# Attention and mixture-of-experts layer on one core: v is transposed by VectorE in 32x32 blocks instead of by TensorE

## The chip, the cores and the metric

One Trainium2 chip, and one of its cores. The metric is the device time of one execution in microseconds (us). The kernel before takes 1060.97 us, the median of 3 runs (1059.65 to 1061.65). The profiled execution, from which every duration below comes, took 1057.24 us; its span in the profile is 1055.5 us.

## The reference, cut to what matters

The kernel computes a layer norm, attention with rotary positions, a second layer norm and a mixture of 8 experts with top-2 routing, all in float32. The change touches only how v reaches the product with the attention weights:

```python
B, L, D = 4, 512, 256;  NQ, NKV, HD = 32, 8, 64      # 4 q heads share one k and one v
proj = layernorm(x) @ W_qkv                            # q, k, v
q, k = rope(q), rope(k);  v = v.reshape(B, L, NKV, HD)
attn = einsum('bqhmd,bkhd->bhmqk', q, k) / 8, masked
w    = softmax(concat([attn, sink]))[..., :-1]         # weights of 512 keys
out  = einsum('bhmqk,bkhd->bqhmd', w, v) @ W_out       # v has 512 rows (keys) of 64
x = x + out;  x = x + ffn(layernorm(x))                # 8 experts, 640 places each
```

## The kernel before

Attention is done in 32 groups (`g`, one batch and one k/v head each), and a group has 16 score tiles of 128 queries by 512 keys (`UNITS`). The main loop `all_periods` has one period per group, of 16 steps `n`. It is software-pipelined: at step `n` of period `g` each engine first does step `n` of group `g`, then step `n - 16` of group `g + 1` (its projection), then step `n + 16` of group `g - 1` (its product with v and its output). So a table entry of -8 stands for step 8 of the period before, and one of 24 for step 8 of the period after. The five engines run their own copies of this list in its order and meet only at semaphores.

In one period, in the order of its steps:

- **TensorE**: at each even step a pair of score tiles (line 1562, 32-bit, two halves of the array at once). A pair waits (line 1558) until VectorE has reduced all tiles but the last one of the pair before. After the pairs of steps 0 and 2 the first two of the next group's three projection chunks (line 1508), after those of steps 4, 6 and 8 the product of the previous group's weights with v (line 1586; 80, 80 and 96 matmuls), after that of step 10 the third chunk (line 1491), after those of steps 12 and 14 the output projection (line 1618).
- **VectorE**: for each tile one mask-scale-minimum instruction (line 1162), at each odd step from 3 on one 32x32-block transposition of two tiles of weights (line 1171), at step 1 the reciprocals (lines 1180 and 1184), at step 9 the division by the sums (line 1191, `heads_sb`), which waits for the last product with v.
- **ScalarE**: the exponentials (line 862), the copies of projection chunks out of PSUM (line 844, `chunk_sb`), and the output copies.
- **GpSimd**: the rotary arithmetic (lines 691, 692, 696) and the split of the weights into two parts.
- **SyncE**: the DMA queue. Per period, in order: reciprocals out and in, the swaps for the rotation of k and of the first q chunk, k doubled, the weights three groups ahead, v out to DRAM (line 505), v in (line 513), the swaps of the second q chunk.

A projection chunk `KV` holds k in partitions 0 to 63 and v in partitions 64 to 127, with one row per feature and the 512 positions along the row. The product needs v with keys in partitions, repeated in four groups of 32 partitions (`v_quads`). Before the change this goes: TensorE transposes v after the score pair of step 8 (`TURN_V_AT`, `turn_v`, line 1526: four transpositions of 64x128 into the bank PROJ); ScalarE copies the bank to `v_next` at step 9 (`v_copy`, line 852); SyncE writes `v_next` to DRAM in one DMA of 128 rows of 1 KB; it reads it back four times into `v_quads`. The third projection chunk (line 1488) waits for ScalarE's copy, since both use the bank PROJ. `v_next` also serves, as `xn1`, for a normalised tile of a later batch in 12 periods (`LATE_PERIODS`, lines 990 to 995).

In periods 0 to 5 VectorE also takes statistics of the later batches (lines 1392 and 1393), in some others the routing's small instructions (`dve_route`). The group before the first period is written out by hand (lines 896 to 916, 1374 to 1381, 1629 to 1640). After the periods, from about 800 us on, come the experts, which the change does not touch.

Of the kernel before, what the change touches and what calls it, by code (L numbers as in the profile page):

```python
# [20 lines left out]
F32 = mybir.dt.float32  # L21
# [5 lines left out]
P = 128  # L27
# [23 lines left out]
BLK = 32  # L51
# [8 lines left out]
def moe_layer(nc, x, w_qkv, w_out, sink, gate_w, w1, b1, w2, b2, rope, out):  # L60
    ctx = ExitStack()
    with ctx:
        slot_rows = nc.dram_tensor("slot_rows", (E * CAP, ROW), F32, kind="Internal").ap()

        v_rows = nc.dram_tensor("v_rows", (P, TPB * HD), F32, kind="Internal").ap()
# [111 lines left out]
        s_v_next = sem("s_v_next")  # L177
# [83 lines left out]
        v_next = sb("v_next", [P, TPB, HD], c=actx)  # L261
        qk_st.append(sb("qk_st1", [P, PAIRS + 1, L], c=actx))
        v_quads = [sb(f"v_quads{i}", [P, TPB, TPB * HD], c=actx) for i in range(2)]
# [13 lines left out]
        xn1 = v_next[:, :, :].rearrange("p t d -> p (t d)")  # L277
# [63 lines left out]
        TURN_V_AT, V_NEXT_AT = -8, -7  # L341
# [97 lines left out]
        def turned_v_bank(g):  # L439

            return PV[0] if g == 0 else PROJ

# [24 lines left out]
        def _(sp):  # L467
# [352 lines left out]
        def _(act):  # L820
# [16 lines left out]
            def chunk_out(g, c):  # L837
# [4 lines left out]
                if c == Q23 and g > 0:  # L842
                    act.wait_ge(s_v_turned, g + 1)
# [4 lines left out]
            def v_copy(g):  # L848
                act.wait_ge(s_v_turned, g + 1)
                if g > 0:  # L850
                    act.wait_ge(s_v_out, g * 16)
                nc.scalar.activation(v_next[:, :, :], turned_v_bank(g)[:, 0:TPB * HD].rearrange("p (c d) -> p c d", d=HD),
                                     ACT.Copy).then_inc(s_v_next, 1)

            def act_step(n, g, j):
                if n in CHUNK_OUT_AT:
                    chunk_out(g, CHUNK_OUT_AT[n])
                if n == V_NEXT_AT:
                    v_copy(g)
# [56 lines left out]
            v_copy(0)  # L916
# [44 lines left out]
            def act_ahead(m):  # L961
# [28 lines left out]
                if m in LATE_NORM_AT:  # L990
                    i = LATE_NORM_AT[m]
                    act.wait_ge(s_late, 1 if i < TPB else 2)
                    act.wait_ge(s_v_out, (LATE_PERIODS[i] + 1) * 16)
                    nc.scalar.activation(xn1, x_sb[:, TPB + i, :], ACT.Identity,
# [111 lines left out]
        def _(dve):  # L1106
# [49 lines left out]

            def dve_step(n, g, j):
# [18 lines left out]
                if n == RECIP_AT:  # L1176
# [7 lines left out]
                    nc.vector.transpose(recip_t[:, :], recip[:, :]).then_inc(s_recip, 1)  # L1184
                if n == HEADS_AT:
# [190 lines left out]
            rotate_q()  # L1376
            dve.wait_ge(s_mask, 1)
# [87 lines left out]
        def _(pe):  # L1465
# [16 lines left out]
            def project(g, j, c):  # L1482
# [4 lines left out]
                else:  # L1487
                    pe.wait_ge(s_v_next, g + 1)
# [25 lines left out]

            def turn_v(g):
                pe.wait_ge(s_chunk_out, g * CHUNKS + (Q01 if g > 0 else KV) + 1)
                if g % NKV == 3 and g > NKV:
                    pe.wait_ge(s_x2T, 2 * (g // NKV))
                if g % NKV == 4 and g > NKV:
                    pe.wait_ge(s_centred, g // NKV)  # L1520
                if g % NKV == 5 and g > NKV:
                    pe.wait_ge(s_place, g // NKV)
                if g - 1 in LATE_PERIODS:
                    pe.wait_ge(s_xT_lo, TPB + LATE_PERIODS.index(g - 1) + 1)
# [276 lines left out]
```

## Time and profile before

| what | value |
|---|---|
| median of 3 runs | 1060.97 us (1059.65 to 1061.65) |
| profiled execution | 1057.24 us, span 1055.5 us |
| TensorE matmul | 1024.9 us busy, 97% of the span |
| TensorE weight load | 720.9 us, 68% |
| VectorE | 926.8 us, 88% |
| ScalarE | 655.0 us, 62% |
| GpSimd | 665.1 us, 63% |
| granted TensorE clock, mean | 0.993 |
| chain that ended last | TensorE 56%, VectorE 37%, issue 3% |

Busy shares are means over the whole span; what ends a wait is read from the chain and from the timelines. The idle time of an engine is printed behind the instruction that ends it, in brackets, with what released it.

### The profile page before, as it was taken

What the parts mean: (1) busy time and instruction counts of PE and PEld (TensorE: products, weight loads), DVE (VectorE), ACT (ScalarE), POOL (GpSimd) and SP (SyncE); (2) the same over time, 40 slices, a digit from 0 to 9 for tenths busy, and PEclk for the clock granted to TensorE, in tenths of its full rate; (3) what the DMA queues carried; (4) which work ended last, traced back from release to release, by engine and by line L of the source; (5) the groups of instructions that cost most, each with busy time, mean ns of one, the idle gap of its engine ahead of it and who ended that gap; (6) DMA issues with size and microseconds to landing.
All of it is one profiled execution on the core that took longest, in us unless ns stands there. A gap on an engine that the chain in (4) does not pass through costs nothing.

```text
span 1055.5 us, 32277 instructions
## 1 busy us (share of the span) xinstructions
PE 1024.9 (97%) x12943; PEld 720.9 (68%) x12943; DVE 926.8 (88%) x1967; ACT 655.0 (62%) x1671; POOL 665.1 (63%) x607
## 2 busy tenths in 40 slices
PE   7899999999999999999999999999988999999996
PEld 4466666666666666666666666666656999999995
DVE  6999999999999999999999999999985787777773
ACT  4666667666667766667776666776663555445551
POOL 6667776777666888666787777777752333333332
PEclk9999999999999999999999999999989999999998
DMA  3534544544333334333334334333424555555521
GB/s 112 142 108 118 137 131 140 132 112 135 93 83 83 96 99 111 99 104 81 80 95 114 100 103 121 98 83 96 119 70 162 119 119 123 117 123 124 101 46 21
DMA packets 155893, 112.10 MB, mean 106 GB/s; under 512 B 76480, under 2 KB 145152, under 8 KB 155616
## 3 DMA queue, kind: packets, MB, share of 16 engines
q1 hardware_dynamic: 137680, 90.03, 33.0%
q0 software_dynamic: 7296, 8.55, 4.8%
q10 hardware_dynamic: 10768, 11.46, 3.6%
q8 instruction: 102, 1.67, 0.7%
q14 instruction: 47, 0.39, 0.1%
HBM read 74.84 MB, written 21.83 MB: 92 GB/s over the span
## 4 chain that ended last, share of the span: by engine, by line
PE 56%; DVE 37%; issue 3%; ACT 1%; POOL 1%; DMA 1%; SPq 0%; POOLq 0%; DVEq 0%; ACTq 0%
PE bank L1586 22%; DVE probs_ring L1162 16%; DVE probs_t L1171 14%; PE bank L1562 10%; PE bank L1739 9%; PE bank L1750 6%; DVE heads_sb L1191 4%; PE bank L1753 3%; PE bank L1618 1%; PE bank L1508 1%; PE bank L1526 1%; PE bank L1533 1%; DVE neg_max L1162 0%; ACT probs_ring L862 0%; PE bank L1491 0%
## 5 line engine op out<-in xcount | busy, mean ns | idle before, releaser
L862 ACT ACTIVATE probs_ring<-probs_ring,neg_max 128x512 f32<-128x512 f32 x512 | 365.8, 717 | 210.3 <-DVE neg_max L1162 209.6
L1162 DVE CUSTOM_DVE_ANT_0 probs_ring<-bank,mask,sink_neg 128x512 f32<-128x512 f32 x512 | 360.1, 737 | 26.6 <-PE bank L1562 25.5
L1171 DVE STREAM_TRANSPOSE probs_t<-probs_ring 128x1024 f32<-128x1024 f32 x256 | 317.5, 1240 | 0.2 <-ACT probs_ring L862 0.2
L1562 PE MATMUL bank<-qk_st 64*128 64x512 f32 x1024 | 281.1, 625 | 11.9 <-DVE neg_max L1162 7.4
L1586 PE MATMUL bank<-probs_t,v_quads 32*64 32x256 f32 x8192 | 247.6, 381 | 0.1
L1586 PEld LDWEIGHTS bank<-probs_t,v_quads 32*64 32x64 f32 x8192 | 179.1, 132 | 76.5 <-issue 48.8
L691 POOL TENSOR_TENSOR chunk_sb<-chunk_sb,rope_sb 128x512 f32<-128x512 f32 (+1 forms) x94 | 120.0, 1276 | 103.9 <-issue 82.7
L810 POOL DMA_INDIRECT out<-expert_sb,slots x40 | 78.8, 1969 | 143.1 <-DVE expert_sb L1428 134.5
L1562 PEld LDWEIGHTS bank<-qk_st 64*128 64x128 f32 x1024 | 85.3, 186 | 77.4 <-DVE neg_max L1162 41.8
L696 POOL TENSOR_TENSOR qk_st<-chunk_sb,swap_sb 128x512 f32<-128x512 f32 (+1 forms) x94 | 120.2, 1279 | 7.4
L1618 PEld LDWEIGHTS bank<-wo_sb,heads_sb 64*128 64x128 f32 x992 | 96.1, 187 | 37.4 <-issue 29.2
L692 POOL TENSOR_TENSOR swap_sb<-swap_sb,rope_sb 128x512 f32<-128x512 f32 (+1 forms) x94 | 120.5, 1281 | 0.0
L1077 ACT ACTIVATE hidden<-bank,b_sb 128x320 f32<-128x320 f32 x128 | 60.6, 525 | 95.7 <-PE bank L1739 95.7
L1618 PE MATMUL bank<-wo_sb,heads_sb 64*128 64x256 f32 x992 | 117.4, 376 | 0.0
L1750 PE MATMUL bank<-w_part,hidden_hi 128*128 128x512 f32 x320 | 114.1, 398 | 0.0
L1508 PE MATMUL bank<-xcur,w_hi 64*128 64x512 f32 x496 | 100.9, 481 | 0.0
L862 ACT ACTIVATION_READ_ACCUMULATOR probs_ring<-probs_ring,neg_max 128x1 f32 x512 | 97.4, 190 | 0.0
L1753 PE MATMUL bank<-w_part,hidden_lo 128*128 128x256 f32 x320 | 90.1, 282 | 0.0
L726 POOL TENSOR_TENSOR x_sb<-x_sb,y_sb 128x512 f32<-128x512 f32 x62 | 79.2, 1277 | 4.5
L1739 PE MATMUL bank<-slots_hi,w_hi 128*128 128x320 f32 x256 | 79.5, 310 | 0.5 <-DVE expert_sb L1428 0.5
L1739 PE MATMUL bank<-slots_lo,w_hi 128*128 128x320 f32 x256 | 79.0, 308 | 0.0
L1739 PE MATMUL bank<-slots_hi,w_lo 128*128 128x320 f32 x256 | 79.0, 308 | 0.0
(191 smaller groups left out, 1342.7 us busy)
## 6 DMA issues: line engine op xcount, KB each, us to landing
v_quads<-v_rows SPq DMA_DIRECT2D x128, 128.0 KB
recip_wide<-recip_rows SPq DMA_DIRECT2D x64, 256.0 KB
w_raw<-in_L_ffn_w SPq DMA_DIRECT2D x14, 1024.0 KB, 7.6
swap_sb<-chunk_sb SPq DMA_DIRECT2D x314, 32.0 KB
w_raw<-in_L_attn_W_qkv SPq DMA_DIRECT2D x32, 256.0 KB, 2.9
slot_rows<-x2T ACTq DMA_DIRECT2D x8, 662.5 KB, 5.8
slots_cut<-slot_rows SPq DMA_DIRECT2D x56, 80.0 KB, 3.0
w_raw<-in_L_attn_W_qkv SPq DMA_DIRECT2D x64, 64.0 KB, 2.7
```

The source lines that it names most:

```text
L691: nc.gpsimd.tensor_tensor(straight, straight, rope_sb[rows, 0, :], ALU.mult).then_inc(s_pool, 1)
L692: nc.gpsimd.tensor_tensor(swapped, swapped, rope_sb[rows, 1, :], ALU.mult).then_inc(s_pool, 1)
L696: nc.gpsimd.tensor_tensor(qk_st[j][rows, PAIRS if c == KV else c - Q01, :], straight, swapped, ALU.add).then_inc(s_rot, 1)
L862: nc.scalar.activation(probs[(g * UNITS + n) % RING][:, :], probs[(g * UNITS + n) % RING][:, :], ACT.Exp, bias=neg_max[j][:, n:n + 1], sca ...
L1162: nc.vector.tensor_tensor_reduce(probs[(g * UNITS + n) % RING][:, :], SCORE[SCORE_OF[n // 2][n % 2]][:, :], mask[:, L - P - t * P:2 * L - ...
L1171: nc.vector.transpose(probs_t[j][:, :, (h // 2) * (2 * P):(h // 2 + 1) * (2 * P)] .rearrange("p b (h q) -> p h b q", h=2)[:, :, :, t * BLK ...
L1562: nc.tensor.matmul(SCORE[SCORE_OF[n // 2][hh]][:, :], qk_st[j][half, h // 2, t * P:(t + 1) * P], qk_st[j][half, PAIRS, :], start=True, sto ...
L1586: ins = nc.tensor.matmul(PV[a][p * HD:(p + 1) * HD, 0:2 * P], v_quads[j][rows, d, c * HD:(c + 1) * HD], probs_t[j][rows, blk, p * 2 * P:(p ...
L1618: ins = nc.tensor.matmul(PV[a][:, 0:D], heads_sb[rows, a, h * P:(h + 1) * P], wo_sb[rows, (g % NKV) * 2 + h, :], start=(half == 0 and h == ...
L1739: ins = nc.tensor.matmul(banks[4 + 2 * (c % 2) + half][:, 0:HALF], w[:, kc, c * P:(c + 1) * P], a[:, at:at + HALF], start=(kc == 0 and m = ...
L1750: nc.tensor.matmul(FFN2[s][:, :], hidden_hi[:, c, s * P:(s + 1) * P], w2_parts[e % 2][:, c, :, :].rearrange("p t d -> p (t d)"), start=(c ...
L1753: ins = nc.tensor.matmul(FFN2[s][:, 0:D], hidden_lo[:, c, s * P:(s + 1) * P], w2_hi[e % 2][:, c, :], start=False, stop=(c == HC - 1))
```

## The change

v is transposed by one VectorE instruction in 32x32 blocks, straight from `chunk_sb[KV]` into partitions 64 to 127 of `swap_sb[KV]`, which nothing else uses. It is placed at step 6 of the period, after that step's tile. Within a block keys and features change places, while the blocks stay: a row of the result is (feature half, key within block) and holds 16 blocks of 32 features. Two DMAs, one per feature half, write it to DRAM as 32 rows (key within block) of 16 x 64, in pieces of 32 numbers. The DMAs back to `v_quads` then move 32 whole rows of 4 KB. TensorE's transposition, ScalarE's copy and their semaphore go; the waits that guarded the bank PROJ move to the third projection chunk; `xn1` becomes a buffer of its own.

```diff
-        v_rows = nc.dram_tensor("v_rows", (P, TPB * HD), F32, kind="Internal").ap()
+        v_rows = nc.dram_tensor("v_rows", (BLK, BLOCKS * HD), F32, kind="Internal").ap()
...
-        v_next = sb("v_next", [P, TPB, HD], c=actx)
+        xn1 = sb("xn1", [P, D], c=actx)
-        v_quads = [sb(f"v_quads{i}", [P, TPB, TPB * HD], c=actx) for i in range(2)]
+        v_quads = [sb(f"v_quads{i}", [P, BLOCKS, HD], c=actx) for i in range(2)]
+        v_turned = swap_sb[KV][HD:P, :]
-        TURN_V_AT, V_NEXT_AT = -8, -7
+        TURN_V_AT = -10
...
 # SyncE, v_out
-                sp.wait_ge(s_v_next, g + 1)
+                sp.wait_ge(s_v_turned, g + 1)
-                sp.dma_start(v_rows, v_next[:, :, :].rearrange("p t d -> p (t d)")).then_inc(s_v_out, 16)
+                for q in range(HD // BLK):
+                    sp.dma_start(v_rows.rearrange("j (b d) -> j b d", d=HD)[:, :, q * BLK:(q + 1) * BLK],
+                                 v_turned[q * BLK:(q + 1) * BLK, :].rearrange("j (b i) -> j b i", i=BLK)
+                                 ).then_inc(s_v_out, 16)
 # SyncE, v_in
-                sp.wait_ge(s_v_out, g * 16 + 16)
+                sp.wait_ge(s_v_out, g * 32 + 32)
-                    sp.dma_start(v_quads[j][a * BLK:(a + 1) * BLK, :, :],
-                                 v_rows.rearrange("(c j) n -> j c n", j=BLK)).then_inc(s_v_in[j], 16)
+                    sp.dma_start(v_quads[j][a * BLK:(a + 1) * BLK, :, :].rearrange("j b d -> j (b d)"),
+                                 v_rows).then_inc(s_v_in[j], 16)
 # ScalarE
-                if c == Q23 and g > 0:
-                    act.wait_ge(s_v_turned, g + 1)
+                if c == KV and g > 0:
+                    act.wait_ge(s_v_turned, g)
-            def v_copy(g):
...
-                nc.scalar.activation(v_next[:, :, :], turned_v_bank(g)[:, 0:TPB * HD].rearrange("p (c d) -> p c d", d=HD),
-                                     ACT.Copy).then_inc(s_v_next, 1)
-                    act.wait_ge(s_v_out, (LATE_PERIODS[i] + 1) * 16)
+                    if i > 0:
+                        act.wait_ge(s_norm_turned, TPB + i)
 # VectorE
+            def turn_v(g):
+                dve.wait_ge(s_chunk_out, g * CHUNKS + KV + 1)
+                if g > 0:
+                    dve.wait_ge(s_v_out, g * 32)
+                nc.vector.transpose(v_turned, chunk_sb[KV][HD:P, :]).then_inc(s_v_turned, 1)
+                if n == TURN_V_AT and g > 0:
+                    turn_v(g)
...
             rotate_q()
+            turn_v(0)
 # TensorE, project(g, j, Q23)
-                    pe.wait_ge(s_v_next, g + 1)
+                    pe.wait_ge(s_chunk_out, g * CHUNKS + Q01 + 1)
+                    if g % NKV == 3 and g > NKV:
+                        pe.wait_ge(s_x2T, 2 * (g // NKV))
...
+                    if g - 1 in LATE_PERIODS:
+                        pe.wait_ge(s_xT_lo, TPB + LATE_PERIODS.index(g - 1) + 1)
-            def turn_v(g):
...
-                for c in range(TPB):
-                    ins = nc.tensor.transpose(turned_v_bank(g)[:, c * HD:(c + 1) * HD],
-                                              chunk_sb[KV][HD:P, c * P:(c + 1) * P],
-                                              identity[HD:P, HD:P])
-                        c, d = divmod(blk, TPB)
-                                                       v_quads[j][rows, d, c * HD:(c + 1) * HD],
+                                                       v_quads[j][rows, blk, :],
```

## Rows read from the trace of the kernel before

**Rows 1.** Chain of waits, part of the page: its shares by line.

```profile
PE bank L1586 22%; DVE probs_ring L1162 16%; DVE probs_t L1171 14%; PE bank L1562 10%; PE bank L1739 9%; PE bank L1750 6%; DVE heads_sb L1191 4%; PE bank L1753 3%; PE bank L1618 1%; PE bank L1508 1%; PE bank L1526 1%; PE bank L1533 1%; DVE neg_max L1162 0%; ACT probs_ring L862 0%; PE bank L1491 0%
```

**Rows 2.** The chain in order of time: start, us on the chain, what.

```profile
366.51 0.24 PE bank L1526 x4
...
372.40 1.16 DVE probs_t L1171
...
381.33 0.71 DVE probs_ring L1162
...
382.10 1.13 PE bank L1562 x4
```

**Rows 3.** Timeline of TensorE, 358 to 367: start, us, line, idle before.

```profile
358.21 1.13 PE L1562 MATMUL bank<-qk_st 64*128 64x512 f32 x4
359.27 1.11 PE L1586 MATMUL bank<-probs_t,v_quads 32*64 32x256 f32 x30
...
365.38 1.13 PE L1562 MATMUL bank<-qk_st 64*128 64x512 f32 x4
...
366.69 2.85 PE L1586 MATMUL bank<-probs_t,v_quads 32*64 32x256 f32 x96
```

**Rows 4.** Every STREAM_TRANSPOSE of VectorE: ns min/median/max, first and last start.

```profile
L1171 DVE STREAM_TRANSPOSE probs_t<-probs_ring x256: 1233/1241/1245, 25.2 to 790.2; 128x1024 f32<-128x1024 f32 x128
...
L1184 DVE STREAM_TRANSPOSE recip_t<-recip x32: 211/211/216, 45.4 to 791.6; 128x32 f32<-128x32 f32 x32
...
L1448 DVE STREAM_TRANSPOSE slots_t<-slots_cut x7: 1503/1505/1516, 836.2 to 1005.4; 128x1280 f32<-128x1280 f32 x7
```

**Rows 5.** Timeline of VectorE: the tile of step 8 and the division, five periods.

```profile
104.83 1.42 DVE L1191 TENSOR_TENSOR heads_sb<-bank,recip_wide 128x256 f32<-128x256 f32 x4
...
272.73 1.42 DVE L1191 TENSOR_TENSOR heads_sb<-bank,recip_wide 128x256 f32<-128x256 f32 x4 [0.49 <-PE bank L1586]
...
297.10 1.42 DVE L1191 TENSOR_TENSOR heads_sb<-bank,recip_wide 128x256 f32<-128x256 f32 x4 [0.23 <-PE bank L1586]
...
345.74 1.42 DVE L1191 TENSOR_TENSOR heads_sb<-bank,recip_wide 128x256 f32<-128x256 f32 x4 [0.31 <-PE bank L1586]
...
366.54 0.75 DVE L1162 CUSTOM_DVE_ANT_0 probs_ring<-bank,mask,sink_neg 128x512 f32<-128x512 f32 x1 [0.73 <-PE bank L1562]
...
369.64 1.42 DVE L1191 TENSOR_TENSOR heads_sb<-bank,recip_wide 128x256 f32<-128x256 f32 x4 [0.51 <-PE bank L1586]
```

**Rows 6.** The chain in period 0 and at its end.

```profile
23.92 0.73 DVE probs_ring L1162
...
46.31 1.13 PE bank L1562 x4
```

**Rows 7.** Timeline of VectorE, the first score tile.

```profile
20.76 0.75 DVE L1162 CUSTOM_DVE_ANT_0 probs_ring<-bank,mask,sink_neg 128x512 f32<-128x512 f32 x1 [0.93 <-PE bank L1562]
```

**Rows 8.** DMA issues: count, KB each, median us from issue to landing.

```profile
slots_cut<-slot_rows SPq DMA_DIRECT2D x56, 80.0 KB, 3.0
...
v_rows<-v_next SPq DMA_DIRECT2D x32, 128.0 KB, 2.5
```

**Rows 9.** Timeline of GpSimd, the rotation of the second q chunk in one period.

```profile
214.26 1.29 POOL L691 TENSOR_TENSOR chunk_sb<-chunk_sb,rope_sb 128x512 f32<-128x512 f32 x1 [2.18 <-DMA swap_sb<-chunk_sb]
...
216.86 1.28 POOL L696 TENSOR_TENSOR qk_st<-chunk_sb,swap_sb 128x512 f32<-128x512 f32 x1
```

**Rows 10.** Timeline of TensorE, the score pair of step 8 in that period.

```profile
219.72 1.13 PE L1562 MATMUL bank<-qk_st 64*128 64x512 f32 x4
```

**Rows 11.** Stretches of the last period: length, busy us by engine, granted clock, DMA.

```profile
762.00:768.00 6.00, 3.44 (x20) 1.67 (x20) 5.96 (x15) 4.58 (x14) 5.14 (x7) 0.90 0.23 67
768.00:774.00 6.00, 6.00 (x86) 2.71 (x84) 3.98 (x8) 5.38 (x11) 1.52 (x2) 0.53 0.30 96
```

**Rows 12.** Timeline of TensorE in the last period, at the lower clock.

```profile
767.62 2.08 PE L1562 MATMUL bank<-qk_st 64*128 64x512 f32 x4 [1.72 <-DVE neg_max L1162]
769.63 4.36 PE L1586 MATMUL bank<-probs_t,v_quads 32*64 32x256 f32 x80
```

More of the change, by code:

```diff
@@ L176, in moe_layer @@
         s_v_turned = sem("s_v_turned")
-        s_v_next = sem("s_v_next")
         s_scores = sem("s_scores")
@@ L276, in moe_layer @@
         ones, before = recip_wide[:, 0, 0:P], heads_sb[:, 0, 0:P]
-        xn1 = v_next[:, :, :].rearrange("p t d -> p (t d)")
+        v_turned = swap_sb[KV][HD:P, :]
         mask_ge = probs_t[1][:, 0:2, :].rearrange("p b q -> p (b q)")[:, 0:MASK_W]
@@ L437, in chunk_bank @@
             return PV[3] if c == KV else PV[1] if c == Q23 and g == 0 else PROJ
-        def turned_v_bank(g):
-            return PV[0] if g == 0 else PROJ
         def turned_bank(half, last):
@@ L846, in chunk_out @@
                                      ACT.Copy).then_inc(s_chunk_out, 1)
-            def v_copy(g):
-                act.wait_ge(s_v_turned, g + 1)
-                if g > 0:
-                    act.wait_ge(s_v_out, g * 16)
-                nc.scalar.activation(v_next[:, :, :], turned_v_bank(g)[:, 0:TPB * HD].rearrange("p (c d) -> p c d", d=HD),
-                                     ACT.Copy).then_inc(s_v_next, 1)
             def act_step(n, g, j):
@@ L857, in act_step @@
                     chunk_out(g, CHUNK_OUT_AT[n])
-                if n == V_NEXT_AT:
-                    v_copy(g)
                 if 0 <= n < UNITS:
@@ L915, in _ @@
             chunk_out(0, Q23)
-            v_copy(0)
             def load_x(b):
@@ L992, in act_ahead @@
                     act.wait_ge(s_late, 1 if i < TPB else 2)
-                    act.wait_ge(s_v_out, (LATE_PERIODS[i] + 1) * 16)
-                    nc.scalar.activation(xn1, x_sb[:, TPB + i, :], ACT.Identity,
+                    if i > 0:
+                        act.wait_ge(s_norm_turned, TPB + i)
+                    nc.scalar.activation(xn1[:, :], x_sb[:, TPB + i, :], ACT.Identity,
                                          bias=bias_late[:, i:i + 1], scale=rstd_late[:, i:i + 1]).then_inc(s_norm, 1)
@@ L1487, in project @@
                 else:
-                    pe.wait_ge(s_v_next, g + 1)
+                    pe.wait_ge(s_chunk_out, g * CHUNKS + Q01 + 1)
+                    if g % NKV == 3 and g > NKV:
+                        pe.wait_ge(s_x2T, 2 * (g // NKV))
+                    if g % NKV == 4 and g > NKV:
+                        pe.wait_ge(s_centred, g // NKV)
+                    if g % NKV == 5 and g > NKV:
+                        pe.wait_ge(s_place, g // NKV)
+                    if g - 1 in LATE_PERIODS:
+                        pe.wait_ge(s_xT_lo, TPB + LATE_PERIODS.index(g - 1) + 1)
                 for kc in range(KC):
@@ L1513, in project_pair @@
                                 ins.then_inc((s_proj_part, s_proj)[second], 1)
-            def turn_v(g):
[L1516 to L1524, printed above, removed]
-                for c in range(TPB):
-                    ins = nc.tensor.transpose(turned_v_bank(g)[:, c * HD:(c + 1) * HD],
-                                              chunk_sb[KV][HD:P, c * P:(c + 1) * P],
-                                              identity[HD:P, HD:P])
-                ins.then_inc(s_v_turned, 1)
             def keep_warm(count, bank, with_rows):
@@ L1592, in pe_step @@
                 if g == 0 and n in WARM_AT:
-                    pe.wait_ge(s_v_next, 1)
                     keep_warm(1, PV[0], x_sb[:, 0:2, :])
@@ L1625, in pe_step @@
                                         ins.then_inc((s_y, s_y_high)[second], 1)
-                if n == TURN_V_AT:
-                    turn_v(g)
             keep_warm(3, SCORE[0], swap_sb[0][:, :])
@@ L1639, in _ @@
             ins.then_inc(s_gate_cols, 1)
-            turn_v(0)
             SLOT_PIECES = [(0, 0, 4), (0, 4, 5), (1, 0, 3), (1, 3, 5)]
```

## The prediction

> **What bounds the kernel now.** I read the chain by line first [rows 1]: TensorE's product with v (line 1586) and VectorE's tile reduction and transposition (lines 1162, 1171) lead it, and TensorE's transposition of v (line 1526) is on it with 1%. Neither engine bounds alone, so the chain in order of time comes next [rows 2]. It alternates once per period. From the score pair of step 4 to the end of the product after step 8 it runs on TensorE, and the transposition of v lies in that half with 0.24 us. Then comes the division, and from there the chain is VectorE back to back until the tile of step 2 (381.33), which releases the pair of step 4 (382.10). TensorE's own work in this second half (third chunk, output projection, next projection) takes about as long; in two periods the chain goes through it instead. The question is therefore: what does the first half gain from losing the transposition on TensorE, and does VectorE have room for its own in that half? The timeline of VectorE answers the second part [rows 5]. In the period at 345 to 370 it is idle 0.73 us ahead of the tile of step 8, which waits for the score pair, and 0.51 us ahead of the division, which waits for the product.
>
> **What TensorE saves.** Score pair to product is 1.06 us without a transposition (358.21 to 359.27) and 1.31 with it (365.38 to 366.69) [rows 3]: 0.25 us a period, 31 periods (the last has no next group). The chain's 0.24 [rows 2] agrees. That is the most that the first half can shorten.
>
> **What VectorE pays.** Before, no block transposition has 512 numbers per partition. 32 numbers take 211 ns, 1024 take 1241, 1280 take 1505 [rows 4]: 1.04 and 1.03 ns a number in between, so 512 take about 0.71 us. On the chain 1024 numbers take 1.16 [rows 2], 0.08 less than their duration, since the next instruction starts that much earlier; so the new one occupies 0.63 us. The ends of the range are 0.13 (the 32-number one less 0.08) and 1.16 (the 1024-number one); the value lies on a straight line through three points, so I take 0.63. It stands after the tile of step 6. The pair of step 8 waits only for that tile, so TensorE does not notice. What waits behind it on VectorE is the tile of step 7, whose exponential is wanted only by the transposition at step 9, two tiles later; then the tile of step 8.
>
> **The sum, period by period.** Let h be the gap ahead of the division plus 0.08, and i the gap ahead of the tile of step 8 plus 0.08. The division comes earlier by 0.25 or by h less what the transposition exceeds i, whichever is smaller; below zero it comes later.
> - 16 periods look like the one at 366.54 [rows 5]: i = 0.81 holds 0.63, h = 0.59, so each gains the full 0.25.
> - One more has some routing work and a smaller gap ahead of step 8 (about 0.37 with the 0.08), which still leaves 0.33 of h: 0.25.
> - Three are like 297.10 [rows 5], with h = 0.31 and room ahead of step 8: 0.25. Together 20 x 0.25 = 5.0 us gained.
> - Three are like 272.73 [rows 5]: statistics fill the gap ahead of step 8, h = 0.57. They lose 0.63 - 0.57 = 0.06 each, 0.2 us.
> - Two are like 345.74 [rows 5]: routing work fills the gap, h = 0.39. They lose 0.24 each, 0.5 us.
> - Periods 1 to 5 are like 104.83, where no gap is printed ahead of the division [rows 5], since VectorE takes statistics there. With about 0.1 us of slack they lose 0.53 each, 2.7 us.
> - In period 0 the chain stays on VectorE from 23.92 to 46.31 [rows 6] and pays all of it: 0.6 us.
>
> Losses 4.0, gains 5.0: 1.0 us less. A delay of the division is passed on whole, because the second half has no idle on VectorE.
>
> **Edits at nothing.** ScalarE loses one copy per period; the chain does not pass through it there. The third projection chunk no longer waits for that copy, but TensorE after the product is not what releases the pair of step 4 [rows 2]; the cover is VectorE's run of eight tiles, and without it the gain would be at most the wait. The waits that move from step 8 to step 10 are for work done earlier and come later than before. The transposition ahead of the first period comes before the mask on VectorE; the first tile then waits 0.93 us for its scores [rows 7], which hides 0.63; uncovered it would cost 0.63 once. The two extra waits of the transposition are for a chunk copied four steps earlier and for DMAs a period old. Reading v back moves the same 128 KB four times; it is wanted more than half a period later.
>
> **The queue of SyncE.** v now leaves in two DMAs with 512 pieces of 128 bytes each, instead of one with 128 pieces of 1 KB that lands in 2.5 us [rows 8]. SyncE stands still until it has landed, and v in and the swaps of the second q chunk queue behind it. The nearest row with such pieces reads 640 of them in 3.0 us [rows 8]. With 0.4 us for the second issue I take a delay of 0.9 us; the ends are 0 and, if pieces have a price each that adds up, several us. Of the ten or so rotations of this chunk that wait for their swaps inside the loop, the one at 214.26 has the least room: it ends at about 218.14 (216.86 plus 1.28) [rows 9], and the pair that needs it starts at 219.72 [rows 10]: 1.6 us. So 0.9 costs nothing.
>
> On this the Trainium skill (DMA: Bandwidth & Descriptors, Specifications) has a rule against the change: transfers under 512 bytes do not reach line rate, since the engine then reads, modifies and writes. No row of this case shows a write of that size and count; with the rule alone the DMA would get slower, but by how much it does not say, and it is weighed below as a rival.
>
> **Forecast.** 1.0 us off the profiled 1057.24 is 1056.2. The median of the runs is 3.7 us above the profiled one; the same 1.0 off 1060.97 gives 1060.0. This is within 0.2% (2.1 us), about what a measurement here can tell from no change. Its own range is 1058.9 to 1063.1.
>
> **The rivals.**
> - VectorE's transposition is absorbed in all periods and TensorE's saving is real in all: 31 x 0.25 = 7.8 us, 1053.2. For it: 20 periods do have the room. Against it: the statistics periods have none [rows 5]. In between, a saving of 0.35 instead of 0.25 (the transposition's start to the product's) gives 7.0 - 4.0 = 3.0 us, 1058.0. Chance 0.15 together.
> - TensorE's clock. In the last period TensorE idles 1.72 us and then has a granted clock of 0.53 for six us [rows 11], the lower of its two levels (1.2 instead of 2.4 GHz); the pair takes 2.08 instead of 1.13, the product 4.36, about twice [rows 12, 3]. That stretch costs about 3 us. If the shifted timing avoids it, 4.0 us are gained: 1057.0, chance 0.13. If the idle that the change adds to TensorE in the statistics periods (0.8 us each) brings two more such stretches, the time is 6.0 - 1.0 us above: 1066.0, chance 0.07. Against both: nothing in that period is changed, and in periods 1 to 5 TensorE stays nearly full.
> - Slower by the transposition's price: if it occupies 1.16 us like the large one, it exceeds i = 0.81 by 0.35. The 16 plain periods nearly bear this (0.24 gained each, 3.9). The one with i = 0.37 loses 0.20, the three like 297.10 lose 0.04 each, and the losing ones now lose 0.59 (three), 0.77 (two), 1.06 (five) and 1.16 (one): 10.1 together. That is 6.2 us slower, 1067.2. Eleven periods pay in full, so the gain is used up from an occupied time of 0.72 us on (0.63 plus 1.0 / 11). For it: two waits ahead of it that the other transpositions do not have. Against it: the three durations on one line [rows 4]. Chance 0.07.
> - Slower by small pieces: SyncE's delay counts from 1.6 us on [rows 9, 10]. At 4 us that period loses 2.4 and about five others with somewhat more room 1 to 1.5 each: 8 us, less 1.0, 1068.0. For it: eight times as many pieces as before. Against it: 640 such pieces land in 3.0 us [rows 8]. The skill's rule stands on this side. Chance 0.08.
>
> **Chances and range.** The forecast has 0.50. Faster by over 0.2%: 0.15 + 0.13 = 0.28. Slower: 0.07 + 0.07 + 0.08 = 0.22. Within 0.2%: 0.50. The range leaves about 0.1 out on each side: 1056.5 to 1065.5.
>
> **What would show it.** Right: a STREAM_TRANSPOSE of 64x512 with 0.71 us, 32 of them; score pair to product 1.06 us at step 8 in all periods; in the period at 366 the gap ahead of the tile of step 8 near 0.1 and ahead of the division near 0.26; the period there shorter by 0.25, those at 80 to 150 longer by about 0.5; the first part of attention later and the rest catching up, the two crossing late. The DMA to `v_rows` landing in about 3 us, and no pair of step 8 that waits for GpSimd. Wrong: a gap ahead of the division of zero in the plain periods (the transposition is dearer than 0.63), a pair of step 8 released by line 696, or slow stretches of the clock at other places.

## The result, and the profile after

The changed kernel takes 1063.43 us (median of 21 runs, 1059.12 to 1073.06), the kernel before, on the same chip, 1059.04 (21 runs, 1054.78 to 1065.39). The ratio is 1.0056, 95% interval 1.0036 to 1.0076: about 6 us slower by the ratio (4.4 by the medians), where 1 us faster was forecast. The time lies inside the range that was given, 1056.5 to 1065.5, but the change goes the other way. The profiled execution took 1062.88 us (span 1061.1, before 1055.5), at a granted clock of 0.992 (before 0.993).

| engine | before | after |
|---|---|---|
| TensorE matmul | 1024.9 us | 1018.7 us |
| VectorE | 926.8 us | 955.9 us |
| ScalarE | 655.0 us | 648.1 us |
| GpSimd | 665.1 us | 663.1 us |

TensorE does 6.2 us less, VectorE 29 more: 22.7 are the 32 transpositions, most of the rest are the stretched instructions below. The chain by line (answers to [rows 1]) has moved towards VectorE: lines 1157 and 1166 are 1162 and 1171 of before, 1575 is 1586, 1150 the new transposition.

```profile
DVE probs_ring L1157 18%; DVE probs_t L1166 16%; PE bank L1575 14%; PE bank L1724 11%; PE bank L1552 8%; PE bank L1735 7%; DVE heads_sb L1188 4%; PE bank L1738 3%; PE bank L1606 1%; DVE swap_sb L1150 1%; PE bank L1514 1%; PE bank L1523 1%; PE bank L1497 1%; DVE neg_max L1157 1%; PE bank L1631 1%
```

The transposition has the duration that [rows 4] gave, 0.71 us (its line's instructions: ns min/median/max):

```profile
L1150 DVE STREAM_TRANSPOSE swap_sb<-chunk_sb x32: 708/708/709, 18.9 to 756.6; 64x512 f32<-64x512 f32 x32
```

The timeline of VectorE in the period that answers to the one at 345 to 370 of before (start, us, line):

```profile
372.17 0.74 DVE L1157 CUSTOM_DVE_ANT_0 probs_ring<-bank,mask,sink_neg 128x512 f32<-128x512 f32 x1
372.84 0.08 DVE L1157 DVE_READ_ACCUMULATOR2_ANT neg_max<- 128x1 f32 x1
372.95 0.71 DVE L1150 STREAM_TRANSPOSE swap_sb<-chunk_sb 64x512 f32<-64x512 f32 x1
373.69 0.75 DVE L1157 CUSTOM_DVE_ANT_0 probs_ring<-bank,mask,sink_neg 128x512 f32<-128x512 f32 x1
374.37 0.08 DVE L1157 DVE_READ_ACCUMULATOR2_ANT neg_max<- 128x1 f32 x1
374.37 1.24 DVE L1166 STREAM_TRANSPOSE probs_t<-probs_ring 128x1024 f32<-128x1024 f32 x1
...
378.35 1.42 DVE L1188 TENSOR_TENSOR heads_sb<-bank,recip_wide 128x256 f32<-128x256 f32 x4 [0.22 <-PE bank L1575]
```

The large transposition starts where the accumulator is read (374.37 and 374.37); the new one starts 0.11 after it (372.84 to 372.95), and the next tile 0.74 after that. It occupies 0.85 us, not the 0.63 of the forecast. The gap ahead of the tile of step 8 is gone, and 0.22 of 0.51 is left ahead of the division. The period is still 0.27 us shorter (division to division).

The largest single loss is somewhere else. The routing instructions of one period, after (VectorE, GpSimd, and the TensorE row that waits), then before (VectorE, GpSimd):

```profile
344.15 1.26 POOL L689 TENSOR_TENSOR chunk_sb<-chunk_sb,rope_sb 64x512 f32<-64x512 f32 x1 [3.26 <-issue]
344.31 1.12 DVE L1354 TENSOR_TENSOR full<-slot_f,slot_end 128x8 f32<-128x8 f32 x1
345.37 1.27 POOL L690 TENSOR_TENSOR swap_sb<-swap_sb,rope_sb 64x512 f32<-64x512 f32 x1
345.47 1.20 DVE L1355 SCALAR_TENSOR_TENSOR scatter_idx<-full,slot_f 128x8 uint32<-128x8 f32 x1
346.59 0.15 DVE L1364 SCALAR_TENSOR_TENSOR top_sum<-gate_sum,top_sum 128x4 f32<-128x4 f32 x1
346.72 1.27 POOL L694 TENSOR_TENSOR qk_st<-chunk_sb,swap_sb 64x512 f32<-64x512 f32 x1
346.99 3.50 DVE L402 TENSOR_TENSOR xn<-gates,top_sum 128x32 f32<-128x32 f32 x1
347.95 1.27 POOL L689 TENSOR_TENSOR chunk_sb<-chunk_sb,rope_sb 128x512 f32<-128x512 f32 x1
349.17 1.26 POOL L690 TENSOR_TENSOR swap_sb<-swap_sb,rope_sb 128x512 f32<-128x512 f32 x1
353.02 1.23 PE L1552 MATMUL bank<-qk_st 64*128 64x512 f32 x4 [4.43 <-DVE neg_max L1157]
```

```profile
340.25 0.17 DVE L1357 TENSOR_TENSOR full<-slot_f,slot_end 128x8 f32<-128x8 f32 x1
340.45 0.17 DVE L1358 SCALAR_TENSOR_TENSOR scatter_idx<-full,slot_f 128x8 uint32<-128x8 f32 x1
340.94 0.19 DVE L403 TENSOR_TENSOR xn<-gates,top_sum 128x32 f32<-128x32 f32 x1
342.18 1.28 POOL L691 TENSOR_TENSOR chunk_sb<-chunk_sb,rope_sb 64x512 f32<-64x512 f32 x1 [4.48 <-issue]
```

Instructions of 0.17 to 0.19 us last 1.12, 1.20 and 3.50. Each ends with a GpSimd instruction that reads SBUF: at 345.43 (344.15 + 1.26 = 345.41), at 346.67 (346.64), at 350.49 (349.17 + 1.26 = 350.43, after three GpSimd instructions without a break). The one at 346.59 fell into the gap before 346.72 and kept its 0.15. Before, GpSimd's rotation began at 342.18, after the last of these. TensorE stands still for 4.43 us, and the period is 5.79 longer.

Two things moved in this period. Counted from the start of the tile of step 6 (342.54 after, 339.33 before), the last routing instruction starts at 4.45 instead of 1.61 (at 2.46 if none before it were stretched, which is the 0.85 of the new transposition), and GpSimd's rotation of k starts at 1.61 instead of 2.85. The 0.85 alone would not have made them meet: 2.46 + 0.19 is still ahead of 2.85.

By periods, counted from division to division (start of line 1191 before, 1188 after), so that "0 and 1" ends with the first division:

| periods | forecast | measured |
|---|---|---|
| 0 and 1 | +1.1 | +1.8 |
| 2 to 5 (statistics) | +2.1 | +2.5 |
| 10, 18, 26 | +0.2 | +0.9 |
| 13, 21 (routing) | +0.5 | +6.3 |
| 29 | -0.25 | +0.7 |
| the 19 others up to 30 | -4.75 | -4.9 |
| 31 and its end | 0 | -2.4 |
| sum | -1.0 | +4.8 |

After the last division come 0.8 us more, which makes the 5.6 between the two spans. The +1.8 of the first line is not all the change's: e6 and e9 below, which leave VectorE's order as it was, have 1.75 and 1.80 there, e4 has -0.13. The start of attention differs that much from one execution to the next.

The -2.4 at the end is the rival on TensorE's clock, on its gaining side: TensorE waits as before (1.83 us, before 1.72), but in the six us from that pair on the granted clock stays at its upper level, 2.4 GHz, where it was 0.53 before (answers to [rows 11, 12]). Why it did not fall is not shown.

```profile
775.00:781.00 6.00, 5.99 (x144) 3.68 (x152) 5.77 (x13) 6.00 (x13) 2.52 (x3) 1.00 0.34 102
```

```profile
775.01 1.13 PE L1552 MATMUL bank<-qk_st 64*128 64x512 f32 x4 [1.83 <-DVE neg_max L1157]
```

### The profile page after: what moved, and what is told of

Same layout as the page of the kernel before. It is cut to its first block, busy times and chain, and to the rows that moved or that the text cites. A ratio compares the mean times of both kernels' runs of the same rounds, so it can differ in the third digit from the quotient of the medians.

```text
span 1061.1 us, 32052 instructions
## 1 busy us (share of the span) xinstructions
PE 1018.7 (96%) x12815; PEld 711.7 (67%) x12815; DVE 955.9 (90%) x1999; ACT 648.1 (61%) x1639; POOL 663.1 (62%) x607
## 4 chain that ended last, share of the span: by engine, by line
PE 48%; DVE 43%; issue 5%; DMA 1%; ACT 1%; POOL 1%; POOLq 0%; SPq 0%; DVEq 0%
DVE probs_ring L1157 18%; DVE probs_t L1166 16%; PE bank L1575 14%; PE bank L1724 11%; PE bank L1552 8%; PE bank L1735 7%; DVE heads_sb L1188 4%; PE bank L1738 3%; PE bank L1606 1%; DVE swap_sb L1150 1%; PE bank L1514 1%; PE bank L1523 1%; PE bank L1497 1%; DVE neg_max L1157 1%; PE bank L1631 1%
## 6 DMA issues: line engine op xcount, KB each, us to landing
slot_rows<-x2T ACTq DMA_DIRECT2D x8, 662.5 KB, 6.4
```

## Experiments

Three theories. **Price**: the transposition occupies 0.85 us on VectorE. **Port**: VectorE's instructions with two SBUF inputs are stretched where they run beside GpSimd's rotation. **Queue**: v leaves in small pieces, and SyncE stands still for it. Each ratio is to runs of the kernel before on the same chip; its medians there were 1060.24 (e1 to e4), 1059.32 (e5 to e8), 1055.88 us (e9 to e12).

**e1: the changed kernel again**

> The changed kernel once more, for a second trace. Port theory: the 5.8 us that the profiled run lost in the period of 354 us are small routing instructions of VectorE with two SBUF inputs (0.17 to 0.19 us each before, 1.12, 1.20 and 3.50 after) that stand still while GpSimd rotates k; whether they meet is a matter of tenths of a microsecond, so this trace should have them in none to three of the three routing periods (near 355, 547 and 739), 1 to 6 us each, and the ratio to the kernel before should be 1.003 to 1.008. Price theory (the transposition alone costs more than its room): the same 2 us above the kernel before in every trace, no stretched small instruction, ratio 1.002. Queue theory (small pieces to DRAM hold SyncE up): a score pair of step 8 released by GpSimd.

1069.31 us, ratio 1.0085 (1.0053 to 1.0116). The same kernel loses its time elsewhere here. Period 13 has one stretched instruction of 0.96 us and costs 1.25; periods 8 and 9 cost 1.5 and 4.6. SyncE, ScalarE's queue, GpSimd and TensorE in period 8:

```profile
208.98 1.27 SPq L501 DMA_DIRECT2D v_rows<-swap_sb  x2
209.54 0.57 ACTq L920 DMA_DIRECT2D slot_rows<-x2T  x1
215.13 1.74 SPq L511 DMA_DIRECT2D v_quads<-v_rows  x4
...
221.77 1.28 POOL L689 TENSOR_TENSOR chunk_sb<-chunk_sb,rope_sb 128x512 f32<-128x512 f32 x1 [5.14 <-DMA swap_sb<-chunk_sb]
...
225.68 1.13 PE L1552 MATMUL bank<-qk_st 64*128 64x512 f32 x4 [1.71 <-POOL qk_st L694]
```

v out to v in takes 6.15 us beside the 662.5 KB of zero rows that ScalarE sends to DRAM; then the swaps, GpSimd and TensorE are late in turn. This is the prediction's queue rival, in two periods.

**e2: the turn one step later**

```diff
-        TURN_V_AT = -10
+        TURN_V_AT = -9
```

> The transposition of v one step later, after the tile and the large transposition of step 7, so behind the routing instructions instead of ahead of them. Port theory: the routing instructions run where they ran before, ahead of GpSimd's rotation of k, none is stretched, and the ratio falls to 1.000 to 1.003. Price theory: the transposition costs the same (0.85 us occupied in the trace after) and no period differs from the changed kernel's other than by 0.1 us; ratio as of the changed kernel. Queue theory: the same as of the changed kernel.

1063.65 us, ratio 1.0021 (0.9993 to 1.0049); the interval lies below that of e1, same chip, one number changed. How much of that is the port's is not shown, since e1's profile lost most at the queue. Periods 13 and 29 cost 0.54 and -0.09, and no routing instruction is stretched in either. Periods 0 to 5 cost 4.6 (4.3 after).

**e3: GpSimd's rotation of k waits for the routing**

```diff
                 pool.wait_ge(s_chunk_out, q + 1)
+                if c == KV and (g - 1) % NKV == 5 and g - 1 > NKV:
+                    pool.wait_ge(s_weights, (g - 1) // NKV)
```

> The changed kernel, but in the three routing periods GpSimd's rotation of k waits until VectorE has written the routing weights. Port theory: no stretched instruction, although nothing of VectorE's order changes; 3 to 5 us less than the changed kernel on average, ratio 1.000 to 1.003; GpSimd starts about 1 us later in three periods, which its room of over 3 us ahead of the next period bears. Price and queue theories: no gain, at best the same as the changed kernel.

1066.18 us, ratio 1.0033 (1.0005 to 1.0061). VectorE's order is that of after, and with GpSimd held back the instruction that took 3.50 us takes 0.19 (VectorE, GpSimd):

```profile
351.53 0.19 DVE L402 TENSOR_TENSOR xn<-gates,top_sum 128x32 f32<-128x32 f32 x1
351.86 1.27 POOL L691 TENSOR_TENSOR chunk_sb<-chunk_sb,rope_sb 64x512 f32<-64x512 f32 x1 [4.43 <-DVE xn L402]
```

Period 13 costs 0.48, 29 -0.13. In this execution (1072.18 us) periods 9 and 10 cost 2.9 and 3.5, with v out to v in at 5.6 and 7.0 us. The interval overlaps that of e1, so it is the trace that shows the port here, not the time.

**e4: the kernel before, routing two steps later**

```diff
-PICK_AT, INDICES_AT, WEIGHTS_AT = 85, 86, 86
+PICK_AT, INDICES_AT, WEIGHTS_AT = 85, 88, 88
```

> The kernel before, with the routing's indices and weights two steps later (step 8 instead of 6), where GpSimd is in its rotation of k in all three routing periods. No transposition of v on VectorE. Port theory: the four or five small two-input instructions stretch to 1 us and more in each of the three periods, and the time rises by 2 to 5 us each, ratio 1.005 to 1.014. Price and queue theories: the same work in another place costs nothing, ratio 0.999 to 1.001.

1073.05 us, ratio 1.0111 (1.0078 to 1.0145). Nothing of v is touched, and the stretching is there, in periods 13, 21 and 29 (+2.8, +3.1, +2.4):

```profile
540.12 0.81 DVE L1357 TENSOR_TENSOR full<-slot_f,slot_end 128x8 f32<-128x8 f32 x1
...
541.04 1.30 DVE L1367 SCALAR_TENSOR_TENSOR top_sum<-gate_sum,top_sum 128x4 f32<-128x4 f32 x1
...
542.66 0.93 DVE L403 TENSOR_TENSOR xn<-gates,top_sum 128x32 f32<-128x32 f32 x1
```

e3 and e4 show the port theory from two sides, one by holding GpSimd back, the other by moving the routing with nothing else changed. The Trainium skill (SBUF — State Buffer, the section on the two sides of SBUF) has it: VectorE with two SBUF inputs and GpSimd take a shared port pair for a whole instruction, and the other "fully blocks". The ends of the stretched instructions above agree with that to 0.06 us.

**e5: e2 with the zero rows eight steps earlier**

```diff
-                if 2 * UNITS <= m < (E + 2) * UNITS and m % UNITS == 13:
+                if 2 * UNITS <= m < (E + 2) * UNITS and m % UNITS == 5:
```

> The changed kernel with the turn at step 7 (as in e2) and ScalarE's issues of the zero rows (662.5 KB each) eight steps earlier in periods 2 to 9, so that they no longer fall beside v's way through DRAM. Queue theory: the time from v's two transfers out to its four in stays at about 3 us, none over 4.5 us in periods 2 to 9, no score pair of TensorE ends its idle on GpSimd's rotation there, and with the stretched routing instructions already gone by step 7 the ratio to the kernel before is 1.000 to 1.002, at or below that of e2 (1.0021). Port theory alone: nothing changes against e2, 1.002. If the long transfers stay although the zero rows are elsewhere, small pieces alone are their cause.

1066.19 us, ratio 1.0069 (1.0045 to 1.0092): a miss, 1.000 to 1.002 was expected. v out to v in stays at 2.9 to 4.0 us in periods 2 to 10, as the queue theory says, but periods 7, 9 and 10 cost 1.3, 0.8 and 1.1 us. The zero rows now go out beside the swaps of k, and GpSimd's rotation of k is late in their place: in period 7 it begins after 5.85 us of idle, before after 2.89. The remedy fails; the collision itself is left to e9 and e10.

Period 13 costs 1.56 us, although the turn stands at step 7 as in e2. One routing instruction is stretched again (GpSimd, VectorE):

```profile
347.84 1.26 POOL L689 TENSOR_TENSOR chunk_sb<-chunk_sb,rope_sb 64x512 f32<-64x512 f32 x1 [3.19 <-issue]
347.90 1.24 DVE L402 TENSOR_TENSOR xn<-gates,top_sum 128x32 f32<-128x32 f32 x1
```

It starts 1.60 us behind the tile of step 6, as in the kernel before; it is the rotation that starts early, at 1.54. In e2 the rotation started at 1.96, and the instruction was through by 1.80. So e2's order escapes only by where the rotation falls.

**e6: the kernel before, v out in small pieces**

```diff
-                sp.dma_start(v_rows, v_next[:, :, :].rearrange("p t d -> p (t d)")).then_inc(s_v_out, 16)
+                for q in range(HD // BLK):
+                    sp.dma_start(v_rows.rearrange("p (t d) -> p t d", d=HD)[:, :, q * BLK:(q + 1) * BLK],
+                                 v_next[:, :, q * BLK:(q + 1) * BLK]).then_inc(s_v_out, 16)
... # the waits for s_v_out count 32 a period instead of 16
```

> The kernel before, with v written to DRAM by two transfers of 512 pieces of 128 bytes each in place of one with 512 pieces of 256 bytes; TensorE's turn stays. Queue theory: the time from v out to v in rises from 2.6 to 3 us and more, now and then to 5 or 6 us beside the zero rows (periods 2 to 9), with one or two periods there longer by 1 to 4 us: ratio 1.000 to 1.004. Port theory and turn's-price theory: ratio 1.000, because no VectorE instruction moves.

1061.29 us, ratio 1.0024 (1.0002 to 1.0045). (The piece before is 1 KB, as in [rows 8]; the 256 bytes of this and of e9's expectation are a slip.) v out to v in takes 3.3 us in the mean (before 2.7), 4 of 32 over 4 us (before 1). The profiled execution shows no loss by the last division (-0.2: +1.8 up to the first division, -2.3 in period 31, 0.35 in all between), so where the 2.5 us of the ratio lie is open.

**e7: the kernel before with VectorE's turn added**

```diff
+                if n == -9 and g > 0:
+                    dve.wait_ge(s_chunk_out, g * CHUNKS + KV + 1)
+                    nc.vector.transpose(swap_sb[KV][HD:P, :], chunk_sb[KV][HD:P, :]).then_inc(s_extra, 1)
... # ScalarE's copy of the next KV chunk waits for s_extra
```

> The kernel before, with VectorE's transposition of the 64x512 v half added at step 7 of each period (its result is used by nothing) and TensorE's transpositions kept. Price theory (0.85 us occupied per period, 0.36 us of routing slack at most where VectorE sets the pace): 20 plain periods unchanged, because TensorE sets them; in the ten or so periods where VectorE is behind, +0.5 to +0.85 us each: in all +4 to +7 us, ratio 1.004 to 1.007, with no stretched routing instruction and no transfer of v over 4 us. If the price hides everywhere the ratio is 1.000, and all the loss of the changed kernel is port and queue.

1065.67 us, ratio 1.0058 (1.0036 to 1.0079). The price alone, with none of TensorE's saving against it, costs as much as the whole change. The 19 other periods cost 0.78 us together; periods 0 to 5 cost 5.1 (2.5 of them up to the first division, where e6 has 1.75 without a turn), and 10, 13, 18, 21, 26 cost 2.0. No routing instruction is stretched.

**e8: no turn at all after group 0**

```diff
-                sp.wait_ge(s_v_turned, g + 1)
+                sp.wait_ge(s_v_turned, 1)
...
-                    act.wait_ge(s_v_turned, g)
+                    act.wait_ge(s_v_turned, 1)
...
-                if n == TURN_V_AT and g > 0:
-                    turn_v(g)
```

> The changed kernel with VectorE's turn done for group 0 alone; the v of all later groups is left out (group 0's is sent each time), transfers and waits stay. Theory of the two prices: TensorE's saving without VectorE's cost: -0.25 us in each of about 31 periods, -7.8 us, ratio 0.992 to 0.994, plus what the small transfers cost in periods 2 to 9 (0 to 4 us); the routing instructions of period 13 aren't stretched, because VectorE isn't pushed late. If TensorE's saving were worth nothing (rival that VectorE sets the pace in the plain periods): ratio 0.999 to 1.000.

The kernel leaves out the v of every group but the first, and SyncE may send v as soon as its queue gets there. 1060.44 us, ratio 1.0003 (0.9977 to 1.0029), where 0.992 to 0.994 was expected: a miss. TensorE's saving is there, 0.24 or 0.25 us in most periods (the 19 others: -4.6). It is lost again in one execution by period 4 (+3.8), at the queue, where v was sent 0.33 us behind the zero rows and took 6.1 us (GpSimd, TensorE):

```profile
123.62 1.28 POOL L689 TENSOR_TENSOR chunk_sb<-chunk_sb,rope_sb 128x512 f32<-128x512 f32 x1 [5.08 <-DMA swap_sb<-chunk_sb]
...
127.52 2.08 PE L1550 MATMUL bank<-qk_st 64*128 64x512 f32 x4 [2.27 <-POOL qk_st L694]
```

One routing instruction (1.15 us at 343.29) is stretched here too, with no transposition on VectorE: GpSimd's rotation starts 1.45 us behind the tile of step 6.

That start sorts the runs in period 13. It is 1.45 to 2.11 us behind the tile in after, e1, e2, e5 and e8, and 2.85 to 3.27 in before and in e6, e7, e9, e10, e11 and e12. (In e3 it is held back.) In each of these runs whose trace has the landing, the rotation starts 0.12 us after the second transfer of k's swap has landed. So the earlier start comes with the change, but not with VectorE's turn (e7: 3.09) and not with the small pieces (e6: 3.27); which part of the change makes that transfer land sooner is open. In periods 21 and 29 the two sets overlap.

**e9: the kernel before, zero rows two steps earlier**

```diff
-                if 2 * UNITS <= m < (E + 2) * UNITS and m % UNITS == 13:
+                if 2 * UNITS <= m < (E + 2) * UNITS and m % UNITS == 11:
```

> The kernel before, with only ScalarE's issues of the zero rows two steps (about 3 us) earlier in periods 2 to 9, so that they are issued within 1.5 us of v's one transfer out (before: v out 1.8 to 3.9 us ahead of them). In e1, e3 and e8 every v out in small pieces issued within 1.1 us of the zero rows, except one at 0.93 and two at 0.74 and 1.11 us ahead, took 4.3 to 7.0 us to v in. Collision theory: those that start in the same microsecond wait for 4 to 7 us here too, with one transfer of 256-byte pieces, and one to three periods get longer by 1 to 5 us: ratio 1.002 to 1.008. If the small pieces are needed for the collision, v out to v in stays under 4 us in all of these periods and the ratio is 1.000.

1056.58 us, ratio 1.0016 (0.9997 to 1.0036), below the 1.002 to 1.008 of the collision theory and not clear of no change. The profiled execution took 1064.37 us, near the top of its ten (1055.12 to 1065.5). In it the long transfers come with large pieces too (SyncE, ScalarE's queue): 5.9 us here, 5.6 and 4.8 in two more periods; periods 8 to 10 cost 0.8, 1.1 and 1.6.

```profile
229.49 0.56 ACTq L932 DMA_DIRECT2D slot_rows<-x2T  x1
231.06 1.45 SPq L505 DMA_DIRECT2D v_rows<-v_next  x1
236.93 1.28 SPq L513 DMA_DIRECT2D v_quads<-v_rows  x3
```

**e10: e9 with e6's pieces**

```diff
 # e9's line, and e6's loop
```

> As e9, with v out in the two transfers of 128-byte pieces of e6. Collision theory: transfers within 1 us of the zero rows take 4 to 7 us, as in e9: ratio 1.003 to 1.010. If pieces alone matter: 3 us everywhere and the ratio of e6, 1.002; if both are needed, this one is slower than e9 by 2 to 6 us.

1071.04 us (4 runs), ratio 1.013 (1.0105 to 1.0155), above what was expected. Each of periods 3 to 10 costs 0.9 to 3.1 us, in all 14.2, and v out to v in takes 3.3 to 6.7. The zero rows alone are worth 0.16%, the pieces alone 0.24 (e6, another chip), both together 1.3: each makes the other worse. On the rule that I weighed in the prediction, the Trainium skill (DMA: Bandwidth & Descriptors, Specifications), that pieces under 512 bytes cost extra work: undisturbed, v out to v in takes 2.9 us in small pieces (e6) and 2.5 in large ones (before), but the second issue alone comes 0.65 us behind the first, and from the last issue on it is 2.3 against 2.5. So undisturbed no run shows a price of the pieces themselves; beside another large write to DRAM it is the difference of e10 to e9.

**e11: the turn on VectorE where it pays**

```diff
+        BUSY = (0, 1, 2, 3, 4, 5, 6, 7, 8, 9, 10, 13, 18, 21, 26, 29)
+        def by_pe(g):
+            return g - 1 in BUSY
...
+                if n == V_NEXT_AT and by_pe(g):
+                    v_copy(g)
...
-                if n == TURN_V_AT and g > 0:
+                if n == TURN_V_AT and g > 0 and not by_pe(g):
...
+                if n == PE_TURN_AT and by_pe(g):
+                    turn_v(g)
```

> TensorE turns v, as before the change, in periods 0 to 10, 13, 18, 21, 26 and 29 (the zero rows' periods and those in which VectorE or ScalarE is late), and VectorE at step 7 in the other 15. Theory of all three costs: the 15 plain periods give 0.24 to 0.25 us each and every loss seen (0.85 us in VectorE-bound periods, stretched routing instructions, long transfers in periods 2 to 9) is gone: -3.5 us, ratio 0.996 to 0.998. If the long transfers or stretched instructions come by chance wherever v goes out in small pieces: ratio 1.000 to 1.003.

1055.69 us, ratio 0.9998 (0.9984 to 1.0012), where 0.996 to 0.998 was expected: a miss, and the interval excludes it. In the profile thirteen of the 15 periods with VectorE's turn gain 0.09 to 0.25 us, 2.9 together, and all of 0 to 10 cost 0.4 together, so the losses seen before are gone. But periods 23 and 24 now cost 0.44 and 0.40, and period 31 with its end 1.5; what delays them is not shown. No version beats the kernel before.

**e12: the transposition by itself**

```diff
             rotate_q()
+            for k in range(4):
+                nc.vector.transpose(probs[k][HD:P, :], rope_sb[HD:P, 0, :])
+            for k in range(4):
+                nc.vector.transpose(probs[k][0:HD, :], rope_sb[0:HD, 0, :])
+            for k in range(4, 6):
+                nc.vector.transpose(probs[k][:, :], rope_sb[:, 0, :])
```

> The kernel before, with ten more transpositions on VectorE between the rotation of group 0 and its first tile, one behind the other and with no wait: four of 64x512 on partitions 64 to 127, four on 0 to 63, two of 128x512; their results are used by nothing. Their starts lie apart by what one occupies. If 0.85 us is the transposition's own price at this size (0.71 and 0.14 that nothing overlaps), the eight small ones start 0.85 us apart on both halves; if 0.63 (the prediction's value) is right behind an equal neighbour and the 0.14 comes from the change of partitions between neighbours, the starts within each four lie 0.63 us apart and only the change from one half to the other costs 0.85. The large ones: 1.16 apart by the rows of before, if the same rule holds.

One execution. VectorE in order of time, GpSimd's last row of the rotation at the end; a row with x2 is two instructions that overlap, each printed from its own start:

```profile
18.63 0.71 DVE L1378 STREAM_TRANSPOSE probs_ring<-rope_sb 64x512 f32<-64x512 f32 x1
19.27 1.27 DVE L1378 STREAM_TRANSPOSE probs_ring<-rope_sb 64x512 f32<-64x512 f32 x2
19.86 1.27 DVE L1378 STREAM_TRANSPOSE probs_ring<-rope_sb 64x512 f32<-64x512 f32 x2
20.45 0.68 DVE L1378 STREAM_TRANSPOSE probs_ring<-rope_sb 64x512 f32<-64x512 f32 x1
21.14 0.70 DVE L1380 STREAM_TRANSPOSE probs_ring<-rope_sb 64x512 f32<-64x512 f32 x1
21.78 1.25 DVE L1380 STREAM_TRANSPOSE probs_ring<-rope_sb 64x512 f32<-64x512 f32 x2
...
22.97 0.66 DVE L1380 STREAM_TRANSPOSE probs_ring<-rope_sb 64x512 f32<-64x512 f32 x1
23.56 0.66 DVE L1382 STREAM_TRANSPOSE probs_ring<-rope_sb 128x512 f32<-128x512 f32 x1
24.75 2.01 DVE L1384 SCALAR_TENSOR_TENSOR mask<-mask,probs_t 128x896 f32<-128x896 f32 x1
23.82 1.99 POOL L696 TENSOR_TENSOR qk_st<-chunk_sb,swap_sb 128x512 f32<-128x512 f32 x1
```

Behind an equal neighbour the starts lie 0.59 to 0.64 us apart, from partitions 64 to 127 to 0 to 63 0.69, and 22.97 to 23.56, from 64 to 128 partitions that both start at 0, again 0.59. So it isn't the size but the change of the first partition that costs 0.10; in the kernel it is paid once going in and once coming out, and 0.64 + 0.10 + 0.11 is its 0.85. The Trainium skill says this (VectorE: DVE Perf Modes, "Two Vector instructions with no wait between them"): an instruction whose input or output starts in another group of 32 partitions than the last one's starts only when all before it have finished. The trace agrees: the first of e12, with no wait ahead of it, starts 0.03 us behind the end of its predecessor, like the kernel's, so the kernel's waits are not the reason. VectorE's last row, with two SBUF inputs beside GpSimd's rotation, lasts 2.01 us; the same instruction takes 1.09 in the changed kernel, where the rotation has not begun. GpSimd's row, which had begun before it, takes 1.99 instead of about 1.28. Here both are stretched, although GpSimd's began first, so a block for the whole of one instruction is not the full account.

## Why the prediction was wrong

By the table of forecast and measured:

- **What TensorE saves**: right. 0.24 to 0.25 us in the plain periods of after and e8; the score pair to the product is 1.05 us (374.34 to 375.39).
- **What VectorE pays**: the duration was right, the occupied time 0.22 us too small. I took the overlap of 0.08 from the large transposition, whose neighbours start at the same partition, and gave it to one that starts at 64 between two that start at 0 (e12). In the plain periods the slack covers it (e7: 0.78 us in 19 periods). Where there is none it shows: +2.5 and +0.9 against 2.1 and 0.2 in periods 2 to 5 and 10, 18, 26, which is 1.1 of the 5.8 us between forecast and profile. The +1.8 against 1.1 in periods 0 and 1 can't be put down to it, since e6 and e9 have it without a turn. This is the third rival at a smaller price. It put the point where the gain is used up at 0.72; 0.85 lies past it, and by its own arithmetic gives (0.85 - 0.72) x 11 = 1.4 us slower.
- **The sum's term for the periods with routing work**: the failed step. The routing work entered the sum as time that fills a gap (h = 0.39, a loss of 0.24 each) and was taken to keep its durations; what GpSimd runs beside it stood at nothing, without a reason. In the profile it was moved 0.85 us later and the rotation started 1.24 earlier, and its short instructions with two SBUF inputs do not bear that: they waited for GpSimd. Periods 13, 21 and 29 cost 7.0 us where +0.3 was forecast (21, in which nothing is stretched, only 0.5 of it), and 13 and 29 together cost 0.35 to 0.45 once either engine's order is changed (e2, e3); in e5, with e2's order, 13 alone costs 1.6 by one stretched instruction. I had read GpSimd only for the waits on it, never for what runs beside it.
- **The queue of SyncE**: "0.9 costs nothing" was right for most periods (v out to v in 3.2 us in the mean, 2.7 before) and wrong by chance. The room of 1.6 us can be passed when v goes out within 1.1 us of the zero rows: of ten such meetings in after, e1, e2, e3 and e8, seven took 4.3 to 7.0 us and three 3.2 to 3.4. The mechanism was listed as a rival at 4 us for every period. What it lacked was the second party: [rows 8] shows the nearest transfer, not what else is under way when v leaves.
- **The clock**: the last period gained 2.4 us in the profiled execution and not in e1 or e2 (+1.6, +1.4). It also differs that much where the old path of v was kept (e6 -2.3, e4 +1.3), so it goes with the execution and not with the change. In the profile this luck hides part of the loss.

How the 6 us divide is only bounded. e2, with neither stretched routing nor long transfers beside the zero rows in its trace, is at 1.0021. If its other executions are like that one, about 2 us belong to price and pieces and some 4 to port and queue, which of the two by chance of the execution. This is an estimate from one set of runs: e5, with the same order, is at 1.0069, and the price alone is 6 us in e7, against a saving of at most 7.8 (31 x 0.25). A placement that avoids the change of partition was not tried.

## What to carry to other kernels

Moving work to an engine with 12% idle moves everything behind it too. List the instructions that will run later and ask of each what it will then run beside: VectorE with two SBUF inputs beside GpSimd, a small DMA beside a large write to DRAM. An instruction's occupied time depends on its neighbours, so take it from start to start beside the neighbours it will have. Where two queues or two engines can meet by chance, price the meeting with its chance, and profile more than one execution: the profiles of the changed kernel, of e1 and of e8 each lost 4 to 6 us in one or two periods, and never in the same ones; and kernels whose work there had not changed differed by up to 1.9 us at the start of attention and by over 3 in its last period.

## What the runs showed of the hardware that I had not expected

- A VectorE instruction of 0.15 to 0.19 us with two SBUF inputs lasts 0.55 to 3.5 us beside GpSimd instructions of 1.27 us (after, e1, e4, e5, e8); it may have to let three of them pass (after).
- VectorE transposes 64x512 and 128x512 in the same time (0.59 us apart), and changing the first partition costs 0.10 (e12).
- v out to v in takes 2.5 us undisturbed in large pieces (before), 2.9 in pieces of 128 bytes with a second issue (e6), and in seven of ten meetings with 662.5 KB of other writes 4.3 to 7.0 (e1, e3, e8).
